# Attention's last two groups: a ring of five banks for the scores, and the last negated maxima turned four steps later

## The chip, the cores and the metric

The kernel runs on one core of one Trainium2 chip. The metric is the device time of one execution in microseconds, and each version is given by the median of its runs. TensorE (PE) does the matrix products and writes only to PSUM, which has eight banks of 128 x 512 float32 values. ScalarE (ACT), VectorE (DVE) and GpSimd (POOL) work beside it, and SyncE (SP) issues the transfers. Each engine takes its own instructions in order; semaphores tie the engines together.

## What is computed

Two layers. The first is causal attention over 4 batches of 1024 tokens, 16 heads of 8 values each, times a gated feed-forward network. The second is a decayed linear attention (retention), times a mixture of experts. Only the first layer's attention is touched. Cut to that, the reference is:

```python
Q = _apply_rope(proj(W_q), positions, sin, cos)
K = _apply_rope(proj(W_k), positions, sin, cos)
V = proj(W_v)
scores = jnp.einsum('bhnd,bhmd->bhnm', Q, K) / jnp.sqrt(jnp.float32(D_K))
scores = jnp.where(causal[None, None], scores, -jnp.inf)
attn = jax.nn.softmax(scores, axis=-1)
head = jnp.einsum('bhnm,bhmd->bhnd', attn, V)
```

## The kernel before

The work of attention is cut into 16 **groups**, x = 0 to 15, each of four heads of one batch. Each group is worked on twice. First come the maxima: PE computes a tile of scores by rows into one of four banks (`mxb`, banks 0 to 3, `for_maximum`, lines 928 to 955) and DVE reduces it to row maxima (line 815). There are 40 such units in a group. Then come the probabilities: PE computes transposed scores, less the maxima, into one of three banks (`st`, banks 4 to 6, `for_products`, lines 957 to 985), ACT takes the exponential from there into `probsB` (line 905), and PE multiplies with the values into bank 7 (`pv`, `products`, lines 997 to 1013). There are 40 **steps** e = 0 to 39 in a group; their number over all groups is n = 40x + e. Steps belong to 12 slots, whose products come five steps after the slot's last step, in a few cases four (`LAG`, `due`). I name a step by its e, and by x where it isn't plain.

Between the two passes the maxima have to reach the other layout. When DVE has all maxima of a group, it combines two tables (line 818), POOL negates and splits them in four small operations (lines 865 to 871), PE turns them in one transpose into the next bank of the maxima's ring (`turn_over`, line 925), DVE copies them to `negB` (line 805), and SP places them with two transfers as extra rows of q (line 727). The steps of the group wait for these at e = 0.

PE's order is written out in the loop at lines 1044 to 1062. In each step of group x stands one unit of maxima beside it, taken from a list (`stream(x)`): units 16 to 39 of group x + 1, then four units of group x + 2, then an entry `(x + 1, None)`, which is the transpose, then twelve more units of group x + 2. So a usual group's transpose stands at e = 28. In group 14 there is no group 16 to work on: the list has only 24 units, the transpose stands at e = 24, and from there to the end of group 15 no maxima are formed. The four banks `mxb` are free after that, but for banks 0 and 1, which take two other jobs in group 15: the first part of the output projection of batch 0 at e = 2 (line 1025, read by DVE at line 832) and the turned rows of its result at e = 20 (line 1033, read by ACT at line 914).

A score of step n waits until ACT has done step n - 3, the last reader of its bank:

```python
if n >= BANKS:
    pe.wait_ge(exp_done, n - BANKS + 1)
bank = st[n % BANKS]
```

ACT does the 40 exponentials, and twice in a group copies bank 7 away (`keep`, line 892): after e = 16 the first half, and after e = 4 of the next group the second. The products that reuse bank 7 wait for the copy. When all engines are through with attention, they meet (line 714), and the stage between the layers begins (lines 1101 onward).

Of the kernel before, what the change touches and what calls it, by code (L numbers as in the profile page):

```python
# [23 lines left out]
ACT = mybir.ActivationFunctionType  # L24
# [614 lines left out]
def attention(nc, A, groups, second, kept_until):  # L639

    NQ = B * QUADS
# [10 lines left out]
    def slot_width(j):  # L652
        c, jt = slots[j]
        return HALF * (c + 1) - max(HALF * c, P * jt)
# [4 lines left out]
    UNITS, SLOTS_B = len(units), len(slots)  # L659
# [3 lines left out]
    RING, BANKS = 4, 3  # L663
    LAG, DEEP = 5, 16

    def stream(x):

        first = [(x + 2, g) for g in range(AHEAD)]
        after = [(x + 1, g) for g in range(AHEAD, UNITS)] + first[:DELAY] + [(x + 1, None)] + first[DELAY:]
        return [u for u in after if u[0] < NQ]  # L670

    prologue = [(0, g) for g in range(AHEAD)] + stream(-1)
    order = prologue + [u for x in range(NQ) for u in stream(x)]
    place_of = {u: n for n, u in enumerate(order)}

    def offset(heads, hq, w):

        return heads.index(hq) * w

    def read_up_to(n):  # L680

        x, r = divmod(n, UNITS)
        return SLOTS_B * x + steps[r][0] + 1

    with Space(nc) as m:
        ps = m.psum("psB")
        mxb = [ps[:, i, :] for i in range(RING)]
        st = [ps[:, RING + i, :] for i in range(BANKS)]
        pv = ps[:, 7, :]
        ident, g2 = second.ident, second.sems  # L690
        choose, hide, hide_later = groups.masks
# [9 lines left out]
        probs = m.sb("probsB", [P, DEEP, HALF])  # L701

        loaded, emptied, slots_cleared = m.sem("constB"), m.sem("emptiedB"), kept_until.slots_cleared
        st_done, exp_done, pv_done = (m.sem(n) for n in ("st_doneB", "exp_doneB", "pv_doneB"))
        out_kept, out_stored = m.sem("out_keptB"), kept_until.heads_stored
        max_done, max_read, combined, split = (m.sem(n) for n in ("max_doneB", "max_readB", "combinedB", "splitB"))
# [7 lines left out]
        with nc.Block() as block:  # L714
# [171 lines left out]
            @block.scalar  # L886
            def _(act):
                def keep(x, c):
                    act.wait_ge(pv_done, SLOTS_B * x + (4 if c == 0 else SLOTS_B))
                    if x:  # L890
                        act.wait_ge(out_stored[c], STORED * x)
                    nc.scalar.copy(out[c][:, :], pv).then_inc(out_kept, 1)

                act.wait_ge(g2["in_loaded"], 16)
                nc.scalar.activation(second.gate[:, :, :], second.u[:, :, :], ACT.Silu).then_inc(g2["gated"], 1)
                act.wait_ge(g2["init"], 2)
                nc.scalar.activation(second.warm[:, :], second.eps[:, :], ACT.Exp)
                for x in range(NQ):
                    for e, (j, heads) in enumerate(steps):
                        n = UNITS * x + e  # L900
                        w = slot_width(j) * len(heads)
                        if n >= DEEP:
                            act.wait_ge(pv_done, read_up_to(n - DEEP))
                        act.wait_ge(st_done, n + 1)
                        nc.scalar.activation(probs[:, n % DEEP, 0:w], st[n % BANKS][:, 0:w], ACT.Exp,  # L905
                                             scale=DH ** -0.5).then_inc(exp_done, 1)
                        if e == last_step[3] + LAG:
                            keep(x, 0)
                        if e == LAG - 1 and x:
                            keep(x - 1, 1)  # L910
                        if x == NQ - 1 and e == TURN_AT + 2:
                            for part, half_of in enumerate(halves):
                                act.wait_ge(g2["turned"], part + 1)
                                nc.scalar.copy(second.xnT[:, 0, half_of], ps[:, part, :]).then_inc(g2["xnT_ready"], 1)
                keep(NQ - 1, 1)

            @block.tensor
            def _(pe):
# [38 lines left out]
                def for_products(x, e):  # L957

                    j, heads = steps[e]
                    c, jt = slots[j]  # L960
                    s = x % QUADS
                    i0 = max(HALF * c, P * jt)
                    w = slot_width(j)
                    n = UNITS * x + e
                    if n >= BANKS:
                        pe.wait_ge(exp_done, n - BANKS + 1)
                    bank = st[n % BANKS]

                    def score(i):
                        hq = heads[i]  # L970
                        r, to = hq % 2, offset(heads, hq, w)
                        ins = nc.tensor.matmul(bank[:, to:to + w], k[half[r], s, hq // 2, jt * P:jt * P + P],  # L972
                                               q[half[r], s, hq // 2, i0:i0 + w], start=True, stop=(jt < 4 * c))
                        if jt < 4 * c:
                            ins.then_inc(st_done, 1)

                    def causal(i, part):
                        r, to = heads[i] % 2, offset(heads, heads[i], w)
                        ins = nc.tensor.matmul(bank[:, to:to + ROWS * (part + 1)], choose[half[r], part, :],  # L979
                                               hide_later[half[r], part, 0:ROWS * (part + 1)], start=False,  # L980
                                               stop=(part == 1))
                        if part == 1 and i == len(heads) - 1:
                            ins.then_inc(st_done, 1)

                    return len(heads), score, None if jt < 4 * c else causal
# [29 lines left out]
                def due(x, j):  # L1015
                    at = last_step[j] + LAG
                    return UNITS * x + (at - 1 if at < UNITS and slot_width(steps[at][0]) == P else at)
# [26 lines left out]
                for x in range(NQ):  # L1044
                    todo = stream(x)
                    pe.wait_ge(neg_placed[x % 2], PLACED * (x // 2 + 1))
                    for e, (j, heads) in enumerate(steps):
                        both = [for_products(x, e)]
                        if todo and todo[0][1] is None:
                            turn_over(todo.pop(0)[0])  # L1050
                        if todo:
                            both.append(for_maximum(*todo.pop(0)))
                        side_by_side(*both)
                        if e == last_step[j]:
                            waiting.append((x, j))
                        if waiting and due(*waiting[0]) <= UNITS * x + e:
                            products(*waiting.pop(0))
                        if x == NQ - 1 and e == PROJECT_AT:
                            output_projection()
                        if x == NQ - 1 and e == TURN_AT:  # L1060
                            turn_rows()
                    assert not todo
# [1355 lines left out]
```

## Time and profile before

| | us |
|---|---|
| median of 3 runs | 1004.39 |
| lowest and highest run | 1002.06, 1005.51 |
| the profiled execution | 999.11 |
| its span, first to last instruction | 997.3 |

The profile is of one execution. Times in its rows are microseconds from the start of the span, so they tell where something lies within 997.3 us. PE's records are modelled at their ends and overlap: how long PE is occupied by a piece is read from the distance between the starts of neighbouring pieces, not from the busy share. ACT's records give true idle time. In a timeline row the bracket at the end tells how long the engine had stood idle before the row, and what released it.

### The profile page before, as it was taken

The page shows a single profiled execution, that of the slowest core. Times are in us where ns is not written, and L with a number is a line of the kernel's source. Part 1 is how long each engine was busy: PE and PEld are TensorE (multiplying, and loading weights), DVE is VectorE, ACT ScalarE, POOL GpSimd, SP SyncE. Part 2 cuts the span into 40 slices and gives each one's busy share as a digit, 9 for nine tenths or more (in the row PEclk, how much of TensorE's full clock was granted, in tenths as well). Part 3 has the DMA queues.
Part 4 walks back from the last instruction along what each step waited for, and adds up shares of the span by engine and source line. Part 5 has one row for each costly group of instructions (what it writes and reads, how often), then busy time and mean ns, then how long its engine had stood idle before and what let it go on. Part 6 is the DMA issues. An engine that isn't in the chain of part 4 may idle for free. (4 is left out here: it accounts for less than half of the span.)

```text
span 997.3 us, 25279 instructions
## 1 busy us (share of the span) xinstructions
PE 869.6 (87%) x9413; PEld 467.9 (47%) x9414; DVE 801.1 (80%) x1691; ACT 726.1 (73%) x1493; POOL 290.6 (29%) x335
## 2 busy tenths in 40 slices
PE   3999899999999999999988699888899999889960
PEld 3666544333334333333334577643444444468850
DVE  6665499999999999999942565399999999928895
ACT  2656408888888888888866445488999999948851
POOL 4875311111111000000012657600444443005560
PEclk9999959999999999999989799969999999979985
DMA  5579861644444353332005678596555443546627
GB/s 168 197 266 333 289 161 42 207 102 101 105 104 107 71 134 83 79 70 41 14 8 145 201 230 230 179 225 143 104 113 90 112 90 54 136 143 206 206 106 254
DMA packets 119385, 140.92 MB, mean 141 GB/s; under 512 B 20109, under 2 KB 82138, under 8 KB 118624
## 3 DMA queue, kind: packets, MB, share of 16 engines
q1 hardware_dynamic: 113888, 127.45, 46.5%
q0 software_dynamic: 5376, 11.85, 4.1%
q8 instruction: 76, 1.25, 0.5%
q14 instruction: 45, 0.37, 0.1%
HBM read 77.63 MB, written 63.25 MB: 141 GB/s over the span
## 5 line engine op out<-in xcount | busy, mean ns | idle before, releaser
L905 ACT ACTIVATE probsB<-psB 128x512 f32<-128x512 f32 (+2 forms) x640 | 310.1, 564 | 87.2 <-PE psB L979 60.1
L815 DVE TENSOR_REDUCE mxB<-psB 128x1 f32<-128x512 f32 (+2 forms) x448 | 257.0, 644 | 10.1 <-PE psB L943 8.4
L972 PE MATMUL psB<-q_groups,k_groups 64*128 64x512 bf16 (+3 forms) x768 | 206.3, 332 | 15.5 <-DVE mxB L815 8.3
L943 PE MATMUL psB<-k_groups,q_groups 64*128 64x512 bf16 (+3 forms) x768 | 216.8, 343 | 3.0 <-PEq L343 1.7
L1010 PE MATMUL psB<-probsB,vB 128*32 128x512 f32 (+3 forms) x1536 | 165.3, 502 | 0.7 <-ACT probsB L905 0.5
L1821 ACT ACTIVATE psD<-psD 128x896 f32<-128x896 f32 (+2 forms) x192 | 153.6, 800 | 8.7 <-PE psD L1875 8.5
L972 PEld LDWEIGHTS psB<-q_groups,k_groups 64*128 64x128 bf16 x768 | 67.5, 94 | 161.0 <-ACT probsB L905 141.2
L1750 DVE TENSOR_REDUCE sumsD<-psD 128x1 f32<-128x128 f32 (+3 forms) x256 | 113.4, 483 | 7.1 <-PE psD L1898 4.9
L1875 PE MATMUL psD<-k_groups,q_groups 64*128 64x512 bf16 (+3 forms) x384 | 103.5, 343 | 13.8 <-ACT psD L1821 5.6
L950 PE MATMUL psB<-hideB,chooseB 64*128 64x128 bf16 (+1 forms) x1024 | 115.1, 210 | 0.0
L815 DVE TENSOR_REDUCE mx2B<-psB 128x1 f32<-128x384 f32 (+2 forms) x192 | 104.6, 596 | 8.5 <-PE psB L950 6.4
L979 PE MATMUL psB<-hide_laterB,chooseB 64*128 64x64 bf16 (+1 forms) x1024 | 109.7, 205 | 0.0
L865 POOL TENSOR_SCALAR partsB<-mxB 128x32 f32<-128x32 f32 x16 | 4.7, 291 | 345.9 <-DVE mxB L818 345.9
L979 PEld LDWEIGHTS psB<-hide_laterB,chooseB 64*128 64x128 bf16 x1024 | 88.5, 96 | 19.8 <-issue 1.3
L950 PEld LDWEIGHTS psB<-hideB,chooseB 64*128 64x128 bf16 x1024 | 92.1, 98 | 9.9 <-issue 3.9
L1761 DVE TENSOR_TENSOR keptD<-psD,causalD 128x512 f32<-128x512 f32 x128 | 82.6, 681 | 0.3 <-PE psD L1894 0.2
L943 PEld LDWEIGHTS psB<-k_groups,q_groups 64*128 64x128 bf16 x768 | 69.0, 95 | 13.4 <-DVE mxB L815 9.1
L2059 POOL DMA_INDIRECT back<-zE,toE x40 | 44.3, 1107 | 86.4 <-DVE zE L2246 76.4
L1875 PEld LDWEIGHTS psD<-k_groups,q_groups 64*128 64x128 bf16 x384 | 29.5, 95 | 81.7 <-ACT psD L1821 47.1
L1898 PE MATMUL psD<-k_groups,q_groups 64*128 64x128 bf16 (+3 forms) x256 | 65.0, 313 | 0.6 <-DVE keptD L1761 0.6
L1894 PE MATMUL psD<-q_groups,k_groups 64*128 64x128 bf16 x512 | 48.9, 225 | 6.5 <-DVE sumsD L1750 6.4
L2137 ACT ACTIVATE hTE<-psE,b1E 128x320 f32<-128x320 f32 x64 | 33.8, 528 | 24.0 <-PE psE L2096 23.4
(233 smaller groups left out, 1531.9 us busy)
## 6 DMA issues: line engine op xcount, KB each, us to landing
v<-vaugA SPq DMA_DIRECT2D x4, 2048.0 KB, 8.7
vB<-v SPq DMA_DIRECT2D x16, 512.0 KB
q_groups<-q SPq DMA_DIRECT2D x32, 200.0 KB
k_groups<-k SPq DMA_DIRECT2D x32, 200.0 KB
back<-emptyB POOLq DMA_DIRECT2D x16, 256.0 KB, 3.8
q<-hiA SPq DMA_DIRECT2D x12, 256.0 KB, 6.7
k<-hiA SPq DMA_DIRECT2D x12, 256.0 KB, 5.7
q_groups<-q SPq DMA_DIRECT2D x32, 96.0 KB
```

Source lines behind the costliest of these rows:

```text
L815: nc.vector.tensor_reduce(dst, src, AX.X, ALU.max).then_inc(max_read, 1)
L905: nc.scalar.activation(probs[:, n % DEEP, 0:w], st[n % BANKS][:, 0:w], ACT.Exp, scale=DH ** -0.5).then_inc(exp_done, 1)
L943: ins = nc.tensor.matmul(bank[:, to:to + w], q[half[r], s, hq // 2, t * P:t * P + P], k[half[r], s, hq // 2, HALF * c:HALF * c + w], start ...
L950: ins = nc.tensor.matmul(bank[:, to - P + ROWS * part:to], choose[half[r], part, :], hide[half[r], part, ROWS * part:P], start=False, stop ...
L972: ins = nc.tensor.matmul(bank[:, to:to + w], k[half[r], s, hq // 2, jt * P:jt * P + P], q[half[r], s, hq // 2, i0:i0 + w], start=True, sto ...
L979: ins = nc.tensor.matmul(bank[:, to:to + ROWS * (part + 1)], choose[half[r], part, :], hide_later[half[r], part, 0:ROWS * (part + 1)], sta ...
L1010: ins = nc.tensor.matmul(pv[VW * hq:VW * hq + VW, HALF - w:HALF], v[:, s, jt, VW * hq:VW * hq + VW], probs[:, (UNITS * x + at) % DEEP, to: ...
L1750: ins = V.tensor_reduce(sums[:, s, unit:unit + 1], src[:, at:at + P * t], AX.X, ALU.add, apply_absolute_value=True)
L1761: V.tensor_tensor(dst[:, :, :, half, :], piece_bank[n % PIECE_RING].rearrange("p (t a i) -> p t a i", t=2, a=2), causal[:, None, None, :]. ...
L1821: nc.scalar.activation(src, src, ACT.Abs, accum_out=sums[:, s, unit:unit + 1]).then_inc(score_read, 1)
L1875: ins = nc.tensor.matmul(score[n % SCORE_RING][:, cols], q[r, s, hq // 2, P * t:P * t + P], k[r, s, hq // 2, cols], start=True, stop=True)
L1898: ins = nc.tensor.matmul(bank[:, at:at + P * t], q[r, s, hq // 2, P * t:P * t + P], k[r, s, hq // 2, 0:P * t], start=True, stop=True)
```

## The change

Two things in `attention`.

From step n = `WIDER` = 588 on (group 14, e = 28) the scores go round five banks, 4, 5, 6, 2 and 3, where before they went round three. `ring_of(n)` says which, and `readers[n]` is how many exponentials must be done before the bank of step n is free. The first use of bank 2 (e = 31) and of bank 3 (e = 32) has no such reader, and waits instead for DVE to have read the whole ring of maxima, the turned one of group 15 included.

In group 14 the transpose of group 15's maxima stands at e = `LATE` = 28 instead of e = 24. The other groups keep theirs, which is also at e = 28.

```diff
+    LATE = 28
+    WIDER = UNITS * (NQ - 2) + LATE
+    ring_of = lambda n: (0, 1, 2)[n % BANKS] if n < WIDER else (0, 1, 2, 3, 4)[(n - WIDER) % 5]
+    readers = [max((p + 1 for p in range(max(0, n - 5), n) if ring_of(p) == ring_of(n)), default=0) for n in range(UNITS * NQ)]
...
-        st = [ps[:, RING + i, :] for i in range(BANKS)]
+        st = [ps[:, i, :] for i in (4, 5, 6, 2, 3)]
...
-                        nc.scalar.activation(probs[:, n % DEEP, 0:w], st[n % BANKS][:, 0:w], ACT.Exp,
+                        nc.scalar.activation(probs[:, n % DEEP, 0:w], st[ring_of(n)][:, 0:w], ACT.Exp,
...
-                    if n >= BANKS:
-                        pe.wait_ge(exp_done, n - BANKS + 1)
-                    bank = st[n % BANKS]
+                    if readers[n]:
+                        pe.wait_ge(exp_done, readers[n])
+                    elif n >= WIDER:
+                        pe.wait_ge(max_read, len(order))
+                    bank = st[ring_of(n)]
...
-                        if todo and todo[0][1] is None:
+                        if todo and todo[0][1] is None and (x < NQ - 2 or e == LATE):
                             turn_over(todo.pop(0)[0])
-                        if todo:
+                        if todo and todo[0][1] is not None:
                             both.append(for_maximum(*todo.pop(0)))
```

What this does to PE's order is seen at two places. The first is group 14, e = 24, where `partsB` are the split maxima, 128x384 a score of the step, `hide_laterB` its causal mask, and `probsB,vB` the products. Before:

```order
L950 MATMUL psB<-hideB,chooseB 128x64
L925 MATMUL psB<-identC,partsB 64x128 [waits splitB,constB,max_readB,exp_doneB]
L972 MATMUL psB<-q_groups,k_groups 128x384
L979 MATMUL psB<-hide_laterB,chooseB 128x64
L979 MATMUL psB<-hide_laterB,chooseB 128x128
L1010 MATMUL psB<-probsB,vB 32x512 [waits exp_doneB]
L1010 MATMUL psB<-probsB,vB 32x512 x3
L972 MATMUL psB<-q_groups,k_groups 128x384 [waits exp_doneB]
```

With the change:

```order
L956 MATMUL psB<-hideB,chooseB 128x64
L980 MATMUL psB<-q_groups,k_groups 128x384 [waits exp_doneB]
L987 MATMUL psB<-hide_laterB,chooseB 128x64
L987 MATMUL psB<-hide_laterB,chooseB 128x128
L1018 MATMUL psB<-probsB,vB 32x512 [waits exp_doneB]
L1018 MATMUL psB<-probsB,vB 32x512 x3
L980 MATMUL psB<-q_groups,k_groups 128x384 [waits exp_doneB]
```

The transpose no longer stands between the last unit of maxima and the score of e = 24. The second place is PE from e = 27 to the products at e = 31. Before:

```order
L972 MATMUL psB<-q_groups,k_groups 128x384 [waits exp_doneB]
L979 MATMUL psB<-hide_laterB,chooseB 128x64
L979 MATMUL psB<-hide_laterB,chooseB 128x128
L972 MATMUL psB<-q_groups,k_groups 128x512 [waits exp_doneB]
L1010 MATMUL psB<-probsB,vB 32x512 [waits exp_doneB]
L1010 MATMUL psB<-probsB,vB 32x512 x3
L972 MATMUL psB<-q_groups,k_groups 128x512 [waits exp_doneB] x3
L1010 MATMUL psB<-probsB,vB 32x384 [waits exp_doneB]
```

With the change:

```order
L980 MATMUL psB<-q_groups,k_groups 128x384 [waits exp_doneB]
L987 MATMUL psB<-hide_laterB,chooseB 128x64
L987 MATMUL psB<-hide_laterB,chooseB 128x128
L931 MATMUL psB<-identC,partsB 64x128 [waits splitB,constB,max_readB,exp_doneB]
L980 MATMUL psB<-q_groups,k_groups 128x512
L1018 MATMUL psB<-probsB,vB 32x512 [waits exp_doneB]
L1018 MATMUL psB<-probsB,vB 32x512 x3
L980 MATMUL psB<-q_groups,k_groups 128x512 [waits exp_doneB] x2
L980 MATMUL psB<-q_groups,k_groups 128x512 [waits max_readB]
L1018 MATMUL psB<-probsB,vB 32x384 [waits exp_doneB]
```

The transpose now stands ahead of the score of e = 28, and the score of e = 31, the first in bank 2, waits for DVE's reads instead of an exponential.

## Rows read from the trace of the kernel before

**Rows 1.** Windows: busy time and instructions of each engine, granted PE clock, DMA.
```profile
core 0: us, PE busy (x) PEld busy (x) DVE busy (x) ACT busy (x) POOL busy (x), PEclk, DMA share, GB/s
300.00:400.00 100.00, 94.09 (x1340) 37.95 (x1336) 95.76 (x178) 85.08 (x178) 6.07 (x19) 1.00 0.45 100
...
504.80:514.40 9.60, 9.29 (x81) 2.85 (x75) 0.00 (x0) 6.39 (x13) 0.00 (x0) 0.76 0.01 3
514.40:539.20 24.80, 22.58 (x223) 9.90 (x223) 6.92 (x29) 20.35 (x43) 1.87 (x2) 1.00 0.46 113
```

**Rows 2.** PE's timeline, group 14, the masks of e = 23 to the score of e = 24.
```profile
start us, us, engine line op out<-in xcount [idle before <-releaser]
498.03 0.19 PE L950 MATMUL psB<-hideB,chooseB 64*128 64x64 bf16 x1
501.16 0.27 PE L925 MATMUL psB<-identC,partsB 128*64 128x128 f32 x1 [2.95 <-POOL partsB L871]
501.37 0.33 PE L972 MATMUL psB<-q_groups,k_groups 64*128 64x384 bf16 x1
```

**Rows 3.** ACT's timeline, exponentials of groups 14 and 15.
```profile
497.71 1.58 ACT L905 ACTIVATE probsB<-psB 128x512 f32<-128x512 f32 x3 [0.56 <-PE psB L979]
501.88 0.49 ACT L905 ACTIVATE probsB<-psB 128x384 f32<-128x384 f32 x1 [2.60 <-PE psB L979]
503.52 1.84 ACT L905 ACTIVATE probsB<-psB 128x384 f32<-128x384 f32 x4 [1.15 <-PE psB L979]
...
516.84 0.98 ACT L905 ACTIVATE probsB<-psB 128x512 f32<-128x512 f32 x2 [1.31 <-PE psB L979]
...
528.47 1.09 ACT L905 ACTIVATE probsB<-psB 128x512 f32<-128x512 f32 x2 [1.58 <-PE psB L979]
```

**Rows 4.** Timelines of POOL and DVE: end of the splitting, copy of the turned maxima.
```profile
500.67 0.25 POOL L871 TENSOR_TENSOR partsB<-partsB,topB 128x32 f32<-128x32 f32 x1
...
501.47 0.28 DVE L805 CAST negB<-psB 64x128 bf16<-64x128 f32 x1 [1.69 <-PE psB L925]
```

**Rows 5.** PE's timeline, group 13, its transpose at e = 28.
```profile
429.66 0.27 PE L925 MATMUL psB<-identC,partsB 128*64 128x128 f32 x1 [0.55 <-ACT probsB L905]
```

**Rows 6.** PE's timeline, group 15: projection, scores and products, turned rows.
```profile
514.28 2.05 PE L1025 MATMUL psB<-w_outC,headTC 128*128 128x128 f32 x16
516.27 0.39 PE L972 MATMUL psB<-q_groups,k_groups 64*128 64x512 bf16 x2
...
516.67 1.07 PE L1010 MATMUL psB<-probsB,vB 128*32 128x512 f32 x8
517.67 0.34 PE L972 MATMUL psB<-q_groups,k_groups 64*128 64x384 bf16 x2
...
526.87 1.09 PE L1033 MATMUL psB<-identC,xnC 128*128 128x128 f32 x8
```

**Rows 7.** Windows of the fall of the clock after e = 23 of group 14.
```profile
498.30:501.20 2.90, 0.04 (x1) 0.07 (x1) 1.44 (x4) 0.98 (x3) 0.92 (x4) 1.00 0.00 0
...
502.70:509.50 6.80, 6.64 (x46) 1.85 (x43) 1.93 (x3) 3.42 (x7) 0.00 (x0) 0.51 0.01 2
```

**Rows 8.** Windows of the start of attention, maxima only.
```profile
117.00:118.70 1.70, 0.07 (x1) 0.00 (x0) 0.69 (x1) 0.00 (x0) 0.00 (x0) 1.00 0.08 30
...
145.00:150.00 5.00, 4.87 (x36) 2.75 (x38) 5.00 (x10) 0.00 (x0) 0.86 (x2) 0.50 0.58 164
```

**Rows 9.** DVE's timeline: normalised rows of the first batch, and after the meeting.
```profile
522.63 2.15 DVE L847 TENSOR_SCALAR xnC<-x1C,momC,rstdC 128x128 f32<-128x128 f32 x8 [2.13 <-POOL rstdC L884]
...
547.46 1.28 DVE L1190 TENSOR_TENSOR x1C<-psC,gateC 128x512 f32<-128x512 f32 x2
```

**Rows 10.** SP's timeline, and DMA rows: KB of one, us from issue to landing.
```profile
532.27 0.46 SPq L776 DMA_DIRECT2D xn<-xnC  x1
...
xn<-xnC SPq DMA_DIRECT2D x1, 512.0 KB, 10.9
o<-outB SPq DMA_DIRECT2D x8, 32.0 KB, 1.7
```

More of the change, by code:

```diff
@@ L678, in offset @@
         return heads.index(hq) * w
+    LATE = 28
+    WIDER = UNITS * (NQ - 2) + LATE
+    ring_of = lambda n: (0, 1, 2)[n % BANKS] if n < WIDER else (0, 1, 2, 3, 4)[(n - WIDER) % 5]
+    readers = [max((p + 1 for p in range(max(0, n - 5), n) if ring_of(p) == ring_of(n)), default=0) for n in range(UNITS * NQ)]
+    assert WIDER % BANKS == 0 and max(n for n, (x, _) in enumerate(stream(NQ - 2))) < WIDER - UNITS * (NQ - 2)
     def read_up_to(n):
```

## The prediction

> **What bounds the kernel now.** I looked first at the windows of a stretch in the middle of attention: DVE is busy 95.76 of 100 us, ACT 85.08, with PE's clock at 1.00 [rows 1]. There DVE's maxima set the pace. The change touches nothing of that. It acts from group 14, e = 24, when DVE has no more maxima, to the meeting at the end of attention. So the next question was who sets the pace there, and I read the timelines of PE and ACT side by side.
>
> PE issues the last masks of e = 23 at 498.03 and then stands still 2.95 us until the transpose at 501.16, released by POOL [rows 2]. POOL's last operation of 0.25 us begins at 500.67 [rows 4], and when it can is fixed by DVE's last maximum. In group 13 the same transpose, four steps later, is preceded by 0.55 us of idleness, and that is put down to ACT, not POOL [rows 5]. ACT meanwhile ends e = 23 at 497.71 + 1.58 = 499.29 and gets e = 24 only at 501.88, after 2.60 us of idleness [rows 3]. Right after, PE's granted clock falls: 1.00 in the standstill, 0.51 from 502.70 to 509.50, the lower of its two levels, 1.2 GHz [rows 7]. Under it PE's work takes about twice as long; at full clock a set of products of 512 columns takes 1.0 us (516.67 to 517.67) [rows 6].
>
> From e = 28 on, neither engine is full. Of the 9.60 us from 504.80 to 514.40 ACT is busy 6.39; of the 24.80 us from 514.40 to 539.20, the last exponential's end, 20.35 [rows 1]. Each long gap on ACT has PE as its releaser [rows 3]: ACT has at most three steps in hand, some 1.6 us (three 512-wide exponentials take 1.58 [rows 3]), and the pieces that PE puts between are 1.0 us (products) and 2.0 us (projection, 514.28 to 516.27) [rows 6]. The idleness ahead of e = 3 (1.31 us) and of e = 21 (1.58 us) follows the projection and the turned rows (526.87, 1.09 us) [rows 3, 6]. So the bound here is the hand-over between PE and ACT, and its floor is ACT's own work.
>
> **The change, part by part.** No instruction of an engine is added or taken away: one transpose moves on PE, with no transfer moved past anything on SP or POOL, and waits change. The replaced waits cost nothing of their own; what counts is when they are met. I follow ACT, because what it can't do earlier the end can't be earlier by. Three terms.
>
> *Term A, up to the exponential of e = 28.* Before, it starts as the fourth of the four from 503.52: they end at 505.36, and a 512-wide one takes some 0.53 to 0.56 us, so about 504.80 [rows 3]. After: the score of e = 24 waits only for the exponential of e = 21, done at about 497.71 + 0.53 = 498.24, so PE issues it at about 498.3, not 501.37. Its slot's predecessor's products follow (1.0 us, to 499.55), then e = 25, 26, 27 one by one, to about 500.3. ACT does e = 24 from 499.3 and, since e = 25 was issued 0.5 us before its exponential can start (501.37 to 501.88 is that distance [rows 2, 3]), e = 25 to 27 from 500.1 to about 501.4. PE meets the transpose at 500.3 and still waits for POOL: it runs at 501.16 as before, since POOL's chain hasn't moved. That is a wait of some 0.9 us, and what is queued behind it is the score of e = 28, and ACT behind that; it costs ACT 0.5 us. The score of e = 28 goes out at 501.36, its exponential starts at 501.85. Term A: 504.80 - 501.85 = **2.95 us**. DVE's copy of the turned maxima ends at 501.75, as before [rows 4], so the scores of e = 31 and 32, issued later, don't wait for it. SP's placing is as late as before too: two issues behind that copy, by about 502.8, and the small transfers land in 1.7 us [rows 10], so at 504.5. Group 15's first score waits for it, and comes at about 507.6 by what follows: 3 us to spare.
>
> *Term B, from e = 28 of group 14 to e = 0 of group 15.* ACT's idleness there was 9.60 - 6.39 = 3.21 us. Not all of it goes, because PE leaves the transpose with nothing in hand. With PE at full clock, products of 1.0 us after the score of e = 28 let the score of e = 29 out at 502.6 and its exponential at 503.05, while ACT is done at 502.4: 0.65 us idle. From there PE can do two steps side by side in 0.25 us or so wherever both banks are free (516.27 to 516.67 holds two 512-wide scores with masks [rows 6]); five banks nearly always give it both. Some 0.2 us more is lost at the products of e = 36. Term B: 3.21 - 0.85 = **2.35 us**.
>
> *Term C, group 15 from e = 1.* ACT's idleness was 24.80 - 20.35 = 4.45 us. The projection of 2.0 us begins with two steps in ACT's hands and more done: I make it 0.65 us of idleness where it was 1.31. The copy of bank 7 after e = 4 and the products behind it leave 0.15. At e = 20 the products must wait for the copy after e = 16, then come 1.0 us of products and 1.03 us of turned rows against four steps, 2.1 us, in ACT's hands: 0.5 us instead of 1.58. After that ACT is never short. Left 1.3; term C: 4.45 - 1.3 = **3.15 us**.
>
> Sum: 2.95 + 2.35 + 3.15 = 8.45 us. After the last exponential the same products and the same copy come, so the meeting moves by as much, and so does all behind it, since the next stage's engines start at the meeting. Bounds: if ACT never waits from e = 28 on, 2.95 + 3.21 + 4.45 = 10.6 us. At the other end B and C give only half of what they are thought to, 2.95 + 2.75 = 5.7 us. I take 8.4, because the remaining waits were placed one by one from rows. Against the profiled execution, 999.11, this gives 990.7. The median of the runs lies 5.28 us over that execution, and the forecast is for a median: 1004.39 - 8.4 = **996.0 us**.
>
> **The clock, a rule and a row.** Term B rests on the clock staying up. PE's clock fell after a standstill of 2.90 us [rows 7]. With the change PE's standstills there are broken up by scores and 1.0 us of products, the longest about 0.9 us. But the row isn't the only one: at the start of attention it fell to 0.50 after a pause of 1.70 us, with maxima at DVE's pace behind it, and was still 0.50 in the window from 145 [rows 8]. The Trainium skill, TensorE: Matmul & The Clock Gate, "Why this matters for your kernels", tells authors to leave no long idle gaps between bursts of matmuls; by that alone the fall goes for certain, and the sum would stand at 8.4. By the second row a shorter pause with sparse work behind it can be enough, and the sum would be that of the first rival. I go with the fall going away, for PE's work from e = 24 on is denser than it was.
>
> **Rivals.** *The fall stays.* 6.8 us at 0.51 hold 3.4 us of PE's work less [rows 7]. PE is the late one up to the projection, so nearly all of it stays: 8.4 - 3.4 = 5.0 us, 999.4 us. For it speaks the wait of 0.9 us at the transpose and the start of attention; against it, two-thirds of the standstill gone. 0.15.
>
> *Something behind takes the gain.* Turned rows need the normalised rows, which are there at 522.63 + 2.15 = 524.78, or 8.5 us after the projection ends [rows 6, 9]. After the change the projection ends at about 510.25, so they are there at 518.75, and PE comes for them at 519.85: 1.1 us to spare. And SP's list in group 15 ends with the issue at 532.27, which lands 10.9 us later, at 543.2, where the next stage's addition at 547.46 needs it: 4.3 us to spare [rows 9, 10], of which the change uses 2 at most. If PE's waits at both, and at the copies of bank 7, eat up B and C but for 0.2 us, A alone is left: 1004.39 - 2.95 - 0.2 = 1001.2 us. 0.08.
>
> *Slower: the clock falls and stays down.* PE's work from e = 28 to the last products is about 24 us at full clock: projection 2.0 and turned rows 1.0 [rows 6], products 12.5 (1.0 for a set of 512 columns [rows 6], narrower ones in proportion, 17 sets), and scores with masks about 8.5, half of them taken to go in pairs, all estimates from the distances in those rows. With the clock at half to the end, as it was at the start of attention still in the window from 145, some 28 us after the pause [rows 8], PE is the bound: 501.4 + 48 = 549.4 where the last exponential ends at 539.20 now, so 10 us later, 1014.5 us. It decides against the change from about 17 us at half clock on, and is slower by over 3 us from 23. Against it: between 514.40 and 539.20 the clock held 1.00 with sparser work than now [rows 1]. 0.03.
>
> *The ring isn't used.* The products at each slot wait for the exponential five steps back, sometimes four, so PE can't be further ahead than that; the ring's fifth bank would be idle at times, but the fourth and fifth steps in hand are what B and C need. That neither matters, and only the moved transpose gives anything, about 3 us less the fall's share: 1000 to 1001. 0.02.
>
> **How the numbers follow.** Forecast 0.72, its own range 993.8 (10.6 us) to 998.7 (5.7 us). The median of a few runs wanders by 1 to 1.5 us, as the three of before do (1002.06 to 1005.51). The range takes in the first rival and that wandering: 992.5 to 1001. A change of 0.3%, 3 us, is about what a measurement of this kernel can tell from none. Faster by more than that: the forecast, nearly all of the first rival and some of the rest, 0.86. Within it: 0.10. Slower: 0.04.
>
> **What the profile of the changed kernel would show.** Term A: the transpose still at about 501.2 with under 1.2 us of idleness before it, the score of e = 24 at about 498.3, the exponential of e = 28 at about 501.9. The clock: 1.00 in all windows from 502 to 510. Term B: ACT idle under 1.2 us from there to e = 0 of group 15, which starts at about 507.6 on PE. Term C: ACT idle about 1.3 us in group 15, its longest gaps 0.5 to 0.7 us ahead of e = 3 and e = 21; last exponential's end near 530.8. The distance from the last copy to the end of the span unchanged within 1 us. The forecast is wrong if the clock is at half for more than 3 us in the stretch, if PE waits over 1 us for the normalised rows, or if the end of attention moves by 8 us and the end of the span doesn't.

## The result

The changed kernel takes 994.63 us in the median, the kernel before 1003.37 us beside it. The ratio is 0.9909, with a 95% interval from 0.9884 to 0.9934: faster by 0.9%, some 8.7 us. Forecast were 996.0 us, from 992.5 to 1001. One of the changed kernel's four runs took 1056.57 us, at a mean granted clock of 0.784 where the others had 0.94; it is in the median of 994.63 (the other three have 994.51), but not in the ratio.

| | before | after |
|---|---|---|
| median, us | 1003.37 | 994.63 |
| span of the profiled execution | 997.3 | 992.7 |
| first splitting operation of POOL, group 15 | 499.87 | 498.95 |
| last copy of bank 7 starts | 540.38 | 531.09 |
| distance between these two | 40.51 | 32.14 |
| from that copy to the end of the span | 456.9 | 461.6 |

The fifth row is the yardstick for all that follows. The change acts between these two points, and what lies ahead of the first shifts both alike (0.92 us here). The distance shrank by **8.37 us**. The spans of the two profiled executions differ by 4.6 us only, because the stages behind attention took 4.7 us less in the one profile of before. The medians don't have that: the median of before, 1003.37 us, is a span of some 1001.6 us (the profiled execution lies 1.8 us over its span), and less 540.4 for the start of the last copy that leaves some 461.2 us, as in the changed kernel. That is an estimate, from the medians and one profile.

PE after the change, from the score of e = 24 on (start, us, engine, line, instruction, idle time before and its releaser; answers to [rows 2] and [rows 6]):

```profile
497.45 0.33 PE L980 MATMUL psB<-q_groups,k_groups 64*128 64x384 bf16 x1
...
497.79 1.07 PE L1018 MATMUL psB<-probsB,vB 128*32 128x512 f32 x8
...
500.25 0.27 PE L931 MATMUL psB<-identC,partsB 128*64 128x128 f32 x1 [0.79 <-ACT probsB L911]
500.45 0.39 PE L980 MATMUL psB<-q_groups,k_groups 64*128 64x512 bf16 x1
500.77 1.07 PE L1018 MATMUL psB<-probsB,vB 128*32 128x512 f32 x8
...
507.26 2.05 PE L1033 MATMUL psB<-w_outC,headTC 128*128 128x128 f32 x16
509.24 0.39 PE L980 MATMUL psB<-q_groups,k_groups 64*128 64x512 bf16 x2
```

The standstill of 2.95 us is gone; 0.79 us of it is left ahead of the transpose. ACT beside it (answers to [rows 3]):

```profile
500.94 0.60 ACT L911 ACTIVATE probsB<-psB 128x512 f32<-128x512 f32 x1 [0.37 <-PE psB L980]
502.25 6.54 ACT L911 ACTIVATE probsB<-psB 128x512 f32<-128x512 f32 x14 [0.72 <-PE psB L980]
509.81 0.98 ACT L911 ACTIVATE probsB<-psB 128x512 f32<-128x512 f32 x2 [1.02 <-PE psB L987]
...
513.05 4.09 ACT L911 ACTIVATE probsB<-psB 128x256 f32<-128x256 f32 x9 [0.53 <-PE psB L987]
...
520.36 1.08 ACT L911 ACTIVATE probsB<-psB 128x512 f32<-128x512 f32 x2 [0.76 <-PE psB L987]
...
522.27 7.63 ACT L911 ACTIVATE probsB<-psB 128x512 f32<-128x512 f32 x17
531.09 0.58 ACT L898 COPY last_outC<-psB 128x512 f32<-128x512 f32 x1 [1.19 <-PE psB L1018]
532.28 1.28 ACT L1321 ACT_TABLE_LOAD   x1 [0.61 <-DMA xC<-x]
```

Fourteen exponentials follow each other without a gap from e = 29 to e = 2 of group 15, and the last seventeen as well. What is left are gaps ahead of e = 28, 29, 3, 8 and 21. The windows (busy time and instructions of PE, PEld, DVE, ACT, POOL, then PE clock, DMA share, GB/s; answers to [rows 1] and [rows 7]):

```profile
497.40:500.20 2.80, 2.01 (x20) 0.76 (x20) 1.43 (x4) 2.25 (x6) 0.92 (x4) 1.00 0.00 0
502.00:510.00 8.00, 8.00 (x98) 4.31 (x99) 3.06 (x6) 6.73 (x15) 0.00 (x0) 1.00 0.02 5
...
500.94:530.01 29.07, 26.82 (x307) 11.10 (x303) 9.68 (x33) 25.92 (x56) 1.87 (x2) 1.00 0.32 76
```

The clock stays at 1.00 where it had been at 0.51.

### The profile page after: what moved, and what is told of

Same layout as the page of the kernel before. It is cut to its first block and busy times, and to the rows that moved or that the text cites. A ratio compares the mean times of both kernels' runs of the same rounds, so it can differ in the third digit from the quotient of the medians.

```text
span 992.7 us, 25280 instructions
## 1 busy us (share of the span) xinstructions
PE 861.7 (87%) x9414; PEld 463.9 (47%) x9414; DVE 800.8 (81%) x1691; ACT 724.9 (73%) x1493; POOL 291.2 (29%) x335
## 5 line engine op out<-in xcount | busy, mean ns | idle before, releaser
L980 PE MATMUL psB<-q_groups,k_groups 64*128 64x512 bf16 (+3 forms) x768 | 202.4, 329 | 14.7 <-DVE mxB L821 8.3
L987 PE MATMUL psB<-hide_laterB,chooseB 64*128 64x64 bf16 (+1 forms) x1024 | 107.7, 204 | 0.0
```

## The experiments

All are compared by the distance from POOL's first splitting operation of group 15 to the start of the last copy of bank 7, in one profile each. Medians, and ratios to the kernel before as it ran beside each set (1002.55 to 1004.87 us), are of the whole kernel.

| kernel | first operation, last copy | distance | median | ratio (95%) |
|---|---|---|---|---|
| before | 499.87, 540.38 | 40.51 | 1003.37 | |
| changed kernel | 498.95, 531.09 | 32.14 | 994.63 | 0.9909 (0.9884 to 0.9934) |
| the same once more | 500.82, 532.96 | 32.14 | 993.19 | 0.9886 (0.9802 to 0.9971) |
| transpose late, three banks | 500.86, 536.36 | 35.50 | 1000.18 | 0.9960 (0.9931 to 0.9989) |
| five banks, transpose at e = 24 | 499.45, 536.59 | 37.14 | 999.23 | 0.9956 (0.9930 to 0.9982) |
| four banks | 499.62, 532.57 | 32.95 | 994.92 | 0.9906 (0.9877 to 0.9935) |
| transpose at e = 30 | 500.42, 532.61 | 32.19 | 993.14 | 0.9897 (0.9867 to 0.9928) |
| the same, shorter wait at e = 31 | 500.80, 532.53 | 31.73 | 996.10 | 0.9921 (0.9891 to 0.9951) |
| pieces in halves | 500.08, 532.83 | 32.75 | 993.95 | 0.9892 (0.9863 to 0.9922) |
| projection at e = 10, turned rows at e = 30 | 500.01, 532.97 | 32.96 | 995.64 | 0.9918 (0.9881 to 0.9955) |
| halves, and transpose at e = 30 | 500.69, 533.49 | 32.80 | 995.64 | 0.9906 (0.9867 to 0.9945) |

The intervals of the eight rows that have both a later transpose and more than three banks overlap, so their medians tell none from another; the distances do, as far as one profile each can (the changed kernel's two agree to 0.01 us).

### Either part alone

First the transpose alone, with three banks kept:

```diff
-                        if todo and todo[0][1] is None:
+                        if todo and todo[0][1] is None and (x < NQ - 2 or e == 28):
                             turn_over(todo.pop(0)[0])
-                        if todo:
+                        if todo and todo[0][1] is not None:
```

> The kernel before with one part of the change alone: the transpose of group 15's maxima stands at e = 28 of group 14, the scores stay in three banks. The yardstick is the distance from POOL's first operation of the last splitting to the start of the last copy of bank 7: before 499.87 to 540.38 = 40.51 us, with the whole change 498.95 to 531.09 = 32.14 us. My theory (the clock's fall comes from the standstill of 2.9 us): no fall between the splitting and group 15, the exponential of e = 28 some 2.9 us earlier, and most of ACT's idleness under the fall gone as well (1.80 us ahead of e = 29 and part of the rest, some 2.3 us), while group 15 keeps its gaps. Distance 35.3 us, time 5.2 us under before. Rival (the clock falls because PE's work is sparse without maxima and with three banks): the fall is there all the same, only 2.9 us are won, distance 37.6 us.

The distance is 35.50 us: 5.01 us less than before. The clock in this kernel, with three banks and no maxima:

```profile
503.00:512.00 9.00, 8.80 (x95) 4.41 (x88) 3.11 (x5) 7.30 (x15) 0.00 (x0) 1.00 0.02 5
```

and ACT's gaps ahead of e = 29, e = 3 and e = 21:

```profile
504.16 2.13 ACT L905 ACTIVATE probsB<-psB 128x512 f32<-128x512 f32 x5 [0.71 <-PE psB L972]
...
512.81 0.98 ACT L905 ACTIVATE probsB<-psB 128x512 f32<-128x512 f32 x2 [1.31 <-PE psB L979]
...
524.44 1.09 ACT L905 ACTIVATE probsB<-psB 128x512 f32<-128x512 f32 x2 [1.58 <-PE psB L979]
```

Group 15 has its old gaps to the hundredth (1.31, 1.58), and the fall is gone although PE has three banks and no maxima, as in the kernel before. So the lack of maxima and the ring of three aren't enough to let the clock fall.

Then the ring alone:

```diff
-                        if todo and todo[0][1] is None and (x < NQ - 2 or e == LATE):
+                        if todo and todo[0][1] is None:
```

> The changed kernel with the transpose back at e = 24, so the ring of five banks alone. My theory: the standstill of 2.9 us and the fall of the clock are there as before, and under the fall PE is the late one, so that a longer ring gives little there; group 15 wins its 2.6 us. Distance from POOL's first splitting operation to the last copy 40.5 - 2.6 = 37.9 us or slightly less, time 2.6 us under before. Rival (the ring gives most of the gain and the moved transpose little): PE makes up for the standstill later by running ahead, distance 34 to 35 us, 5 to 6 us under before.

The distance is 37.14 us, 3.37 less than before and 0.8 less than I expected. The standstill is back, and with it the fall:

```profile
500.75 0.27 PE L931 MATMUL psB<-identC,partsB 128*64 128x128 f32 x1 [2.95 <-POOL partsB L877]
```

```profile
502.30:509.10 6.80, 6.64 (x46) 1.88 (x43) 1.92 (x3) 3.42 (x7) 0.00 (x0) 0.50 0.01 2
```

Under it the ring gives next to nothing, as ACT's timeline shows: the same 1.80 us ahead of e = 29 as before, and e = 32 starts 9.76 us after POOL's first operation where it was 9.79. The 0.8 us that I had left out are won between e = 32 and e = 2 of group 15, where eleven exponentials now follow each other (two gaps of 0.33 and 0.20 us stood there before). In what follows the gaps are nearly those of the changed kernel:

```profile
506.70 1.57 ACT L911 ACTIVATE probsB<-psB 128x512 f32<-128x512 f32 x3 [1.80 <-PE psB L980]
509.21 5.07 ACT L911 ACTIVATE probsB<-psB 128x256 f32<-128x256 f32 x11 [0.93 <-PE psB L987]
515.32 0.98 ACT L911 ACTIVATE probsB<-psB 128x512 f32<-128x512 f32 x2 [1.04 <-PE psB L987]
```

The two parts add up: 5.01 + 3.37 = 8.38 us, against 8.37 together. In this stretch the fall is there wherever the standstill of 2.95 us is, and gone wherever that is gone; the other kernels below have neither, with a clock of 1.00 throughout from 495 to 530. The length of a pause alone doesn't decide it, though. Elsewhere in the profile of before PE stands still 2.21 us ahead of 111.14 and the clock stays at 1.00 until the next pause, 1.69 us ahead of 118.75, behind which it is at 0.50; and in retention it is at 0.50 from 667 and from 691 on, after pauses of 1.20 us (ahead of 664.34) and 1.10 us (ahead of 689.94). What a pause of another length would do at this place was not tried.

### Four banks

```diff
+    ring_of = lambda n: (0, 1, 2)[n % BANKS] if n < WIDER else (0, 1, 2, 3)[(n - WIDER) % 4]
```

> The changed kernel with a ring of four banks (4, 5, 6, 2) from e = 28 of group 14 on. My theory: the gaps on ACT behind the projection and the turned rows grow by one step each, from 1.02 to 1.5 us ahead of e = 3 and from 0.76 to 1.2 us ahead of e = 21; distance 32.1 + 1.0 = 33.1 us, time 1 us over the changed kernel. Rival (the fifth bank lies idle since the products wait for the exponential four or five steps back): distance 32.1 to 32.3 us, gaps as in the changed kernel.

The distance is 32.95 us, 0.81 more. The fifth bank isn't idle, so the total is nearly as I had it, but not the places: the gap ahead of e = 3 is 1.09 us instead of 1.02, that ahead of e = 21 is 0.76 in both. The loss comes in small pieces where products of a whole slot stand between scores: 14 exponentials from e = 29 take 6.75 us instead of 6.54, a gap of 0.21 us opens ahead of the last eleven, and the last seventeen take 0.31 us more.

```profile
502.93 6.75 ACT L911 ACTIVATE probsB<-psB 128x512 f32<-128x512 f32 x14 [0.72 <-PE psB L980]
...
523.23 2.66 ACT L911 ACTIVATE probsB<-psB 128x512 f32<-128x512 f32 x6
526.10 5.28 ACT L911 ACTIVATE probsB<-psB 128x512 f32<-128x512 f32 x11 [0.21 <-PE psB L980]
```

### What is left ahead of the transpose

```diff
-                        if todo and todo[0][1] is None and (x < NQ - 2 or e == LATE):
+                        if todo and todo[0][1] is None and (x < NQ - 2 or e == 30):
```

> The changed kernel with the transpose at e = 30 of group 14 instead of e = 28, the ring of five from e = 28 as it is. My theory: PE's 0.79 us of idleness ahead of the transpose is POOL's chain and now lies under other work, and ACT's gaps of 0.37 us ahead of e = 28 and 0.72 us ahead of e = 29 shrink by 0.8 us in all; distance 32.1 - 0.8 = 31.3 us. Rival (what PE wins there it loses at the next hand-over, since PE's own work from e = 24 to the projection is the bound): the gap ahead of e = 3 doesn't shrink and distance stays within 0.2 us of 32.1.

The distance is 32.19 us: nothing won, which is the rival's number, though the run after this one shows another reason than the rival's. The score of e = 28 did go out earlier, 0.91 us after POOL's first operation (501.33 to 500.42) instead of 1.50 (500.45 to 498.95). But PE's scores of e = 30 and 31 then take long:

```profile
501.33 0.39 PE L980 MATMUL psB<-q_groups,k_groups 64*128 64x512 bf16 x1 [0.40 <-ACT probsB L911]
...
502.96 0.30 PE L931 MATMUL psB<-identC,partsB 128*64 128x128 f32 x1
503.19 0.83 PE L980 MATMUL psB<-q_groups,k_groups 64*128 64x512 bf16 x2
503.95 0.85 PE L1018 MATMUL psB<-probsB,vB 128*32 128x384 f32 x8
504.74 0.23 PE L980 MATMUL psB<-q_groups,k_groups 64*128 64x128 bf16 x1
```

The score of e = 31, the first in bank 2, waits for all 656 reads of the maxima's ring, the last of which is DVE's copy of the turned maxima at 503.29. The next kernel asks it to wait for the 655 reads ahead of that copy only, which take in all of bank 2's:

```diff
-                        pe.wait_ge(max_read, len(order))
+                        pe.wait_ge(max_read, len(order) - (1 if e == 31 else 0))
```

> The kernel with the transpose at e = 30, and the first score in bank 2 (e = 31) waiting only for the 655 reads of the units of maxima, not for DVE's copy of the turned ones, which lie in bank 3. With the transpose at e = 30 the distance didn't shrink (32.19 us), and there DVE's copy starts at 503.29, in the midst of the scores of e = 30 and 31 (503.19, two in 0.83 us, where two or three side by side take 0.4 to 0.6). My theory: that wait, put on the path by moving the transpose so late, ate what was won ahead of e = 28 (that score goes out 0.9 us after POOL's first splitting operation instead of 1.5). Without it PE is 0.3 us ahead at e = 32, and since PE's own work is the bound up to e = 7 of group 15, the distance falls to 31.9 us. Rival (ACT's exponentials, not PE, are behind the gaps there): distance 32.2 us, no change.

The distance is 31.73 us, the shortest of all and 0.46 less than with the long wait. The two scores now go side by side, and the first narrow score comes 3.86 us after POOL's first operation (504.66 to 500.80) instead of 4.32 (504.74 to 500.42), which is the whole 0.46. In the changed kernel it is 4.13, so of the 0.8 us that I had hoped for from the later transpose 0.4 are there:

```profile
503.56 0.39 PE L980 MATMUL psB<-q_groups,k_groups 64*128 64x512 bf16 x2
503.88 0.85 PE L1018 MATMUL psB<-probsB,vB 128*32 128x384 f32 x8
504.66 0.23 PE L980 MATMUL psB<-q_groups,k_groups 64*128 64x128 bf16 x1
```

So that wait was new, it came from the change, and it costs nothing where the transpose stands at e = 28: there DVE's copy is done at 500.84 and the scores of e = 29 to 31 go from 501.77 on, three in 0.60 us. The whole kernel's time tells this version apart neither from the changed kernel nor from the one with the long wait (996.10 us in its median).

### The pieces in between

The projection in halves after e = 2 and e = 3, and the turned rows after e = 20 and 21:

```diff
-                        if x == NQ - 1 and e == PROJECT_AT:
-                            output_projection()
-                        if x == NQ - 1 and e == TURN_AT:
-                            turn_rows()
+                        if x == NQ - 1 and e in (PROJECT_AT, PROJECT_AT + 1):
+                            output_projection(e - PROJECT_AT)
+                        if x == NQ - 1 and e in (TURN_AT, TURN_AT + 1):
+                            turn_rows(e - TURN_AT)
```

> The changed kernel with the projection given in two halves after e = 2 and e = 3 of group 15 and the turned rows in two halves after e = 20 and e = 21; the work is the same. My theory (PE's own work is the bound from e = 24 of group 14 to the products at e = 7 of group 15, which wait for a copy): the gap of 1.02 us ahead of e = 3 shrinks, but only the 0.2 us that PE waits at e = 7 is won; at the turned rows PE is ahead of ACT, and the gap of 0.76 us ahead of e = 21 shrinks by 0.5 us for good. Distance 32.1 - 0.7 = 31.4 us. Rival (each gap on ACT is lost time by itself): both gaps shrink by what half the piece takes, 1.0 and 0.5 us, distance 30.6 us.

The distance is 32.75 us, 0.61 more, and both theories miss. The gap ahead of e = 3 is gone, but in its place stand 0.84 us ahead of e = 4 and 0.47 us at the copy behind it. PE shows why:

```profile
508.39 1.16 PE L1033 MATMUL psB<-w_outC,headTC 128*128 128x128 f32 x8
509.49 0.39 PE L980 MATMUL psB<-q_groups,k_groups 64*128 64x512 bf16 x1
509.88 1.16 PE L1033 MATMUL psB<-w_outC,headTC 128*128 128x128 f32 x8
510.98 0.33 PE L980 MATMUL psB<-q_groups,k_groups 64*128 64x384 bf16 x1
511.32 1.07 PE L1018 MATMUL psB<-probsB,vB 128*32 128x512 f32 x8
```

From 508.39 to the products at 511.32 are 2.93 us; in the changed kernel it is 507.26 to 509.65, 2.39 us. Cut in two, the projection takes 1.10 + 1.10 us instead of 1.98, and the scores of e = 3 and e = 4 go one by one, in 0.39 and 0.34 us, where they had gone side by side as "x2" in 0.41 us. That PE is the late one here is confirmed by the loss: 0.54 us more of PE's time are nearly the whole 0.61 us of distance.

Projection and turned rows moved as wholes:

```diff
-        SCALED, PROJECT_AT, TURN_AT = QUADS + 3, 2, 20
+        SCALED, PROJECT_AT, TURN_AT = QUADS + 3, 10, 30
```

> The changed kernel with the projection at e = 10 instead of e = 2 of group 15 and the turned rows at e = 30 instead of e = 20. My theory: the gap ahead of e = 3 only moves to e = 11, at about 1 us, since PE has no lead there either, but the turned rows at e = 30 fall where PE waits for ACT anyway (0.81 us at e = 28), so the gap of 0.76 us ahead of e = 21 goes: distance 31.3 us. Behind the meeting the store of the normalised rows, issued some 5 us later, may be waited for: up to 1 us back. Rival (the pieces cost ACT the same wherever they stand): distance 32.1 us.

The distance is 32.96 us, 0.82 more, and again both theories miss. The gap ahead of e = 21 is gone, as I had thought, but the one that moved grew to 1.71 us, since two of the steps in ACT's hands there are narrow, and around the turned rows at e = 30 ACT waits 0.19 and 0.57 us after all:

```profile
515.75 3.17 ACT L911 ACTIVATE probsB<-psB 128x512 f32<-128x512 f32 x6 [1.71 <-PE psB L987]
```

The halves together with the transpose at e = 30, with the long wait at e = 31:

> The halves of the projection and the turned rows together with the transpose at e = 30. My theory: what each wins adds up only as far as PE has no work of its own to do there: distance 31.3 us. Rival (the moved transpose is worth 0.8 us once the projection no longer covers it up): 30.6 us. At the meeting ACT waits for the load of x by then (0.1 us in the changed kernel), so anything won in attention beyond the changed kernel is partly given back: the start of the next stage's first table load after the last copy grows from 1.19 us by what is won.

The distance is 32.80 us, the halves' 32.75 but for 0.05, so both theories miss here too. ACT's first table load comes 1.09 us after the last copy starts, no later than before, so nothing was given back at the meeting.

### The spread behind attention

> The changed kernel once more, beside the others of this set. My theory: the distance from POOL's first operation of the last splitting to the start of the last copy of bank 7 is a fixed property of the program, 32.1 us again within 0.1, and the spread from run to run comes from the stages behind attention: retention's products, first to last, took 224.9 us in the profile of before, 225.9 after, and up to 232.4 in the others, the experts 79.6 to 85.0 us. Rival: the distance itself wanders by 1 us or more. Time 993 to 996 us, 8 to 9 us under before.

The distance is 32.14 us again. Ahead of it POOL's first operation wanders from 498.95 to 500.86 us over the eleven profiles, 1.9 us. The larger part of the spread is behind the meeting. The products of the second layer's retention and the experts' activations, by first and last start (line, instructions, shortest/median/longest ns, first and last start in us), in the kernel before, in the changed one, and, for retention alone, in the kernel with the ring alone:

```profile
L1875 PE MATMUL psD<-k_groups,q_groups x384: 216/373/631, 645.5 to 870.4; 64*128 64x512 bf16 x177, 64*128 64x384 bf16 x14, 64*128 64x256 bf16 x1
L2137 ACT ACTIVATE hTE<-psE,b1E x64: 527/527/531, 879.5 to 959.1; 128x320 f32<-128x320 f32 x64
```

```profile
L1883 PE MATMUL psD<-k_groups,q_groups x384: 216/372/631, 635.5 to 861.4; 64*128 64x512 bf16 x178, 64*128 64x384 bf16 x13, 64*128 64x256 bf16 x1
L2145 ACT ACTIVATE hTE<-psE,b1E x64: 519/527/529, 869.9 to 954.3; 128x320 f32<-128x320 f32 x64
```

```profile
L1883 PE MATMUL psD<-k_groups,q_groups x384: 216/386/631, 640.2 to 872.6; 64*128 64x512 bf16 x176, 64*128 64x384 bf16 x14, 64*128 64x256 bf16 x2
```

Retention: 224.9, 225.9 and 232.4 us. Experts: 79.6 and 84.4 us, so the profile of before is short in the experts, not in retention. From the last copy to the end of the span the eleven profiles have 456.9 (before), 461.6, 461.3, 460.1, 467.2, 460.0, 458.1, 461.8, 462.6, 458.3 and 461.0 us, in the order of the table. The profile of before is the shortest of them all. The text of these kernels is the same in those stages. The slowest goes with more half clock at retention's start: over its first 75 us the granted clock was 0.84 before and 0.75 with the ring alone.

```profile
645.50:720.50 75.00, 65.29 (x763) 30.71 (x768) 72.76 (x177) 65.30 (x145) 15.27 (x22) 0.84 0.70 162
```

```profile
640.20:715.20 75.00, 66.47 (x694) 30.01 (x696) 67.54 (x167) 60.71 (x133) 12.93 (x19) 0.75 0.70 157
```

That the clock is the cause and not a companion of slower transfers wasn't shown.

## Why the prediction was right, point by point

**The sum.** Forecast 8.4 us less, measured 8.37 us in the distance and 8.7 us in the medians. The median came out 1.4 us under the forecast, 1.0 of it because before has 1003.37 us in four runs where the forecast started from 1004.39 in three. The three terms can be read from the two timelines, by the exponential of e = 28 and the end of that of e = 2. In the kernel before:

```profile
514.44 1.09 ACT L905 ACTIVATE probsB<-psB 128x512 f32<-128x512 f32 x2 [0.20 <-PE psB L979]
```

| | forecast | measured |
|---|---|---|
| A, to the exponential of e = 28 | 2.95 | 4.90 - 1.99 = 2.91 |
| B, to the end of e = 2 of group 15 | 2.35 | 15.66 - 9.84 - 2.91 = 2.91 |
| C, from there to the end | 3.15 | 8.37 - 5.82 = 2.55 |

(4.90 is 504.77 less 499.87, where the trace has the exponential of e = 28 alone at 504.77, for 0.60 us; 1.99 is 500.94 less 498.95; 15.66 is 514.44 + 1.09 less 499.87, and 9.84 is 502.25 + 6.54 less 498.95. The forecast drew the line between B and C at e = 0; it had nothing to win in e = 1 and 2, so its terms stand as they are.)

**Term A** came out as written, since POOL's chain holds the transpose where it was. The 0.79 us ahead of it are put down to ACT by the trace, not to POOL as I had it: the score of e = 28 also waits for the exponential of e = 25, that wait stands ahead of the transpose in PE's order, and with the transpose moved to e = 30 0.40 us of it remain. But POOL's last operation ends at 499.75 + 0.25 = 500.00 and the transpose comes 0.25 us later, as it did before (500.92 and 501.16). So some 0.4 us of the wait are ACT's, and the rest POOL's.

**Terms B and C** were right in their sum, 5.46 for 5.5 us, and off in their parts by some 0.6 us each that cancelled. That the sum fits so closely is luck. Two errors stand behind it. The gaps that I left were too small: ahead of e = 29, 3, 8 and 21 I had 0.65, 0.65, 0.15 and 0.5 us, measured are 0.72, 1.02, 0.53 and 0.76; only the 0.2 us at the products of e = 36 didn't come. That is 0.9 us too few. The steps that failed most are those at e = 3 and e = 8. At e = 3 ACT has 1.53 us of work left when the projection starts (507.26 to 508.79), where my 0.65 us wanted some 1.9. At e = 8 the products at e = 7 wait for the copy after e = 4, PE works in order, and so a longer ring lets no score past them; the gap is 0.53 us with three banks and with five. Against this, I had taken ACT's busy time as fixed. It is not: 6.39 + 20.35 = 26.74 us for 56 instructions before, 25.92 for 56 after. An exponential of 512 columns takes 0.60 us alone, but two that follow each other take 1.08 to 1.09 us together, since the second starts before the first has ended; with fewer gaps more of that is hidden. That gave back 0.8 us.

**The clock.** The fall went with the standstill. The Trainium skill's advice against long idle gaps between bursts of matmuls (TensorE: Matmul & The Clock Gate, "Why this matters for your kernels") agrees with these traces at this place: the standstill of 2.95 us has the fall behind it in both kernels that have it, the 0.8 us has none. In my own argument for it, denser work, the longer ring had a part, and that part wasn't needed: with three banks the clock held as well. The rival in which the fall stays had 0.15, and I had priced the fall too high, at 3.4 us. From the exponential of e = 28 to the start of e = 1 are 514.44 - 504.77 = 9.67 us with it and 510.41 - 502.85 = 7.56 us without, both with three banks: 2.1 us. With five banks it is 2.1 us as well, from e = 28 to the end of e = 2. The first 2.9 us aren't all the pause's either: under the fall e = 25 goes from its score to its exponential in 0.75 us (502.77 to 503.52), at full clock in 0.52 (498.79 to 499.31), so some 0.2 us of term A is likely the clock's. No run has the standstill without the fall.

**The rivals.** Turned rows were not waited for: PE had them when it came. The loads behind the meeting were nearer than I had reckoned. I had looked at the store that lands last, with 4.3 us to spare; but the load of x lands at 523.20 + 8.9 = 532.1, and ACT's table load waits for it from 531.67 on, 0.61 us instead of 0.50. In the changed kernel's second profile it doesn't (0.50 us). So that load is within 0.1 us of the path now, and an attention that ended earlier without its copy after e = 16 moving too would wait for it. The ring is used, to its fifth bank. Nothing slower appeared.

**The signs.** Two of the signs that I gave came out otherwise, one in full and one by half. From the last copy to the end of the span I wanted the same within 1 us, and it is 4.7 us more; and I called the forecast wrong if the end of attention moved by 8 us and the end of the span didn't. Attention's end moved by 9.3 us, 8.4 without what lies ahead of it, and the span's by 4.6. By the profiles alone that sign is half met. The medians (8.7 us) and the second profile of the changed kernel (461.3 us) speak for a short execution of before rather than for a loss behind attention. Both signs compared single executions over stages that wander by 10 us.

**The range** of 992.5 to 1001 holds the median. The 5.28 us between the profiled execution and the median of before were taken over to the forecast as they were. For the median that was right, because that execution was a short one behind attention; for the profiled execution it gave 990.7 us, and measured are 994.76.

## What to carry to other kernels

Where an ordered engine stands still for a value that another makes, look at what it could do first; here one transpose four steps later was worth 5.0 us alone, some 2.9 up to the exponential of e = 28, mostly the pause, and 2.1 behind it, where the clock no longer fell. A longer ring between two engines pays where long pieces sit between short ones, but not past a wait that the producer itself must pass in order. And a wait that is put down for several banks at once should name the reads of its own bank: it costs nothing until something else moves.

## What the runs showed of the hardware

A stretch whose instructions wait for each other and not for large transfers can repeat to 0.01 us: the distance was 32.14 us in both profiles of the changed kernel, with the DMA engines 0.32 busy beside it, and gaps of 1.31 and 1.58 us came again unchanged in another kernel. Of the spread of the whole, 10.3 us (456.9 to 467.2) lie behind attention, where transfers are heavier (0.70 over retention's first 75 us) and the clock comes and goes, and 1.9 us ahead of the stretch. Which of the two makes the spread wasn't shown.

A pause of PE and a fall of its clock go together at the place of this change, but no one length of pause fits the rows: 2.95 us had the fall behind it and 0.79 us none, while in other stages 1.10 us had one and 2.21 us had none.

A piece of PE's work of 1.98 us takes 1.10 + 1.10 us when a score stands between its halves, and two scores that go side by side in 0.41 us take 0.39 and 0.34 us alone. Here cutting a long piece on PE into short ones cost more than it evened out.
